# A buffer for each pair of heads for P's 512-column tiles, and three scratch tiles folded into others

## The reference

```
qkv    = xn @ w_qkv.T + b_qkv                 # 16 heads of 32
scores = q @ k.T / sqrt(32), causal           # 512 x 512 for each head
out    = softmax(scores) @ v                  # "AV"
attn   = out @ w_out.T + b_out
g, u   = (xn @ gate_w.T) * gate_s, (xn @ up_w.T) * up_s      # 1408 wide
ffn    = ((silu(g) * u) @ down_w.T) * down_s
```

## Time and profile before

| | |
|---|---|
| median of 3 runs | 1948.21 us (1943.7 to 1949.09) |
| the profiled execution | 1939.12 us |
| its span | 1937.2 us |
| granted TensorE clock | 0.993 |
| busy: PE / PEld / DVE / ACT / POOL | 96% / 63% / 78% / 74% / 65% |
| chain that ended last: PE / DVE / SP's queue / DMA / ACT | 66% / 9% / 8% / 7% / 5% |

### The profile page before, as it was taken

How to read it: one execution, slowest core, us unless ns; L and a number is a source line. 1 busy time by engine, 2 the same in 40 slices (tenths; PEclk the granted TensorE clock), 3 DMA queues, 4 the chain that set the end, 5 groups by cost and what they waited for, 6 DMA issues and landing times.

```text
span 1937.2 us, 44142 instructions
## 1 busy us (share of the span) xinstructions
PE 1864.4 (96%) x14978; PEld 1221.9 (63%) x14978; DVE 1503.4 (78%) x4516; ACT 1441.2 (74%) x4263; POOL 1255.9 (65%) x1799
## 2 busy tenths in 40 slices
PE   6899999999999999999999999999999999999996
PEld 4566665666666666675656666666566666766663
DVE  4878778787777878778777787877778777787785
ACT  4787777878777787777867778677687777778674
POOL 5775857757676675857748576575666656576462
PEclk9999999999999999999999999999999999999999
DMA  9978969788797977979789797887968778797685
GB/s 222 168 161 161 183 131 204 141 164 167 142 190 134 183 157 156 183 132 194 133 150 177 135 196 124 164 157 137 184 128 172 144 141 179 131 182 133 123 159 99
DMA packets 818551, 305.93 MB, mean 158 GB/s; under 512 B 756176, under 2 KB 793168, under 8 KB 818320
## 3 DMA queue, kind: packets, MB, share of 16 engines
q1 hardware_dynamic: 796176, 240.79, 69.3%
q0 software_dynamic: 22144, 62.27, 12.0%
HBM read 55.59 MB, written 16.78 MB: 37 GB/s over the span
## 4 chain that ended last, share of the span: by engine, by line
PE 66%; DVE 9%; SPq 8%; DMA 7%; ACT 5%; issue 3%; POOL 1%; POOLq 0%; ACTq 0%; DVEq 0%
PE bank L248 66%; DMA pt<-phl 6%; SPq L897 5%; DVE phl L552 3%; ACT phl L451 3%; SPq L904 2%; DVE bank L542 1%; ACT bank L459 1%; DVE res L579 1%; DVE small L516 1%; DVE xhl L692 1%; ACT small L447 0%; DVE ft L562 0%; SPq L889 0%; DVE fh L567 0%
## 5 line engine op out<-in xcount | busy, mean ns | idle before, releaser
L552 DVE SCALAR_TENSOR_TENSOR phl<-bank,small,phl 128x512 f16<-128x512 f32 (+3 forms) x1024 | 526.3, 545 | 200.3 <-ACT phl L451 197.4
L459 ACT ACTIVATE bank<-bank,small 128x512 f32<-128x512 f32 (+3 forms) x1024 | 516.0, 505 | 153.7 <-DVE small L542 152.9
L542 DVE CUSTOM_DVE_ANT_0 bank<-bank,mask 128x512 f32<-128x512 f32 (+3 forms) x1024 | 483.2, 503 | 146.0 <-PE bank L248 143.3
L451 ACT ACTIVATE phl<-bank,small 128x512 f16<-128x512 f32 (+3 forms) x1024 | 500.0, 531 | 110.7 <-DMA pt<-phl 100.3
L248 PE MATMUL bank<-xnT,wg 128*128 128x256 f16 x2816 | 367.6, 273 | 4.5 <-DVE fh L567 4.5
L248 PE MATMUL bank<-xnT,wu 128*128 128x256 f16 x2816 | 365.8, 273 | 0.0
L248 PE MATMUL bank<-xnT,wqkv 128*128 128x512 f16 x1536 | 352.4, 379 | 0.0
L248 PE MATMUL bank<-wd,ht 128*128 128x512 f16 x1408 | 316.1, 380 | 0.3 <-POOL ht L763 0.3
L248 PEld LDWEIGHTS bank<-xnT,wg 128*128 128x128 f16 x2816 | 263.9, 98 | 67.0 <-DVE fh L567 5.4
L248 PEld LDWEIGHTS bank<-xnT,wu 128*128 128x128 f16 x2816 | 276.0, 98 | 32.4
L248 PE MATMUL bank<-stk 96*128 96x512 f16 (+3 forms) x1024 | 245.6, 301 | 31.3 <-DVE phl L552 28.4
(11 more groups left out here) (97 smaller groups left out, 2181.7 us busy)
## 6 DMA issues: line engine op xcount, KB each, us to landing
stk<-qkp SPq DMA_DIRECT2D x768, 64.0 KB, 2.1
res<-in_x_dram POOLq DMA_DIRECT2D x64, 256.0 KB, 4.8
xin<-in_x_dram POOLq DMA_DIRECT2D x60, 256.0 KB, 4.7
out_dram<-res POOLq DMA_DIRECT2D x60, 256.0 KB, 3.4
pt<-phl SPq DMA_TRANSPOSE x512, 4.3
xin<-in_gate_dram POOLq DMA_DIRECT2D x11, 256.0 KB, 3.4
xin<-in_up_dram POOLq DMA_DIRECT2D x11, 256.0 KB, 3.4
xin<-in_down_dram POOLq DMA_DIRECT2D x11, 256.0 KB, 4.0
```

The lines of the kernel that those rows point to most:

```text
L451: i = eng.activation(phl[qt][:, j % 2, 0], pb[:, off:off + W], ACT.Copy, scale=st_r[:, c:c + 1])
L459: i = eng.activation(pb[:, off:off + W], pb[:, off:off + W], ACT.Exp, bias=st_m[:, c:c + 1], scale=-1.0, accum_out=st_s[:, c:c + 1])
L542: i = eng.tensor_tensor_reduce(out=bk[:, off:off + W], in0=bk[:, off:off + W], in1=mask[:, 512 - W:512], scale=-(32.0 ** -0.5) / (QS * QS) ...
L552: i = eng.scalar_tensor_tensor(phl[qt][:, j % 2, 1], pb[:, off:off + W], st_r[:, c:c + 1], phl[qt][:, j % 2, 0], ALU.mult, ALU.subtract)
```

## The change

It has three parts, and the order of every engine's work stays as it was but for the loads of x.

1. The 512-column size of `phl` gets a second tile, so that each pair has its own, with its own semaphore. `high` of a 512-column unit now waits for the turn of its own pair in the group before, and `av` waits on five landing semaphores instead of four.
2. `dtmp` becomes another name for `q32[0]`. `drain_av` additionally waits until every `down_add` ahead of it is done, `down_scale` until every `split_av` ahead of it is done.
3. `xs32` is gone: `scaled` normalises in place in `xin`. A buffer of `xin` is free for the next load only after the low half (L692) and no longer after `scaled`; the load is issued three steps ahead of the statistics (four for the one at step 3 of the first batch).

The second tile takes as many bytes of a partition (4096) as `dtmp` and `xs32` give back.

```diff
-    phl = [sb(f"phl{i}", [128, 2, 2, 128 * (i + 1)], F16) for i in range(4)]
+    phl = [[sb(f"phl{i}", [128, 2, 2, 128 * (i + 1)], F16)] for i in range(3)]
+    phl.append([sb(f"phl3_{p}", [128, 2, 2, 512], F16) for p in range(2)])
-    dtmp = sb("dtmp", [128, 512], F32)
+    dtmp = q32[0]
-    xs32 = sb("xs32", [128, 512], F32)
-    d_pt = [sem(f"d_pt{i}") for i in range(4)]
+    d_pt = [[sem(f"d_pt{i}")] for i in range(3)] + [[sem(f"d_pt3_{p}") for p in range(2)]]
+    avs_ahead = {bt: sum(n < m for n in av_at) for m, bt in d_at.items()}
+    ds_ahead = {G: sum(n < m for n in d_at) for m, G in av_at.items()}
-    later = [(n - 4, ("norm", *v)) for n, v in norm_at.items()] + ...
+    later = [(n - (4 if n < 4 else 3), ("norm", *v)) for n, v in norm_at.items()] + ...
-        xin_reader[i] = {"norm": (v_xs, 4 * what[1] + what[-1] + 1), ...
+        xin_reader[i] = {"norm": (v_xl, 4 * what[1] + what[-1] + 1), ...
+    part = lambda qt, j: phl[qt][j // 2 if qt == 3 else 0]
...
         def av(G):
-            for qt in range(4):
-                w.wait_ge(d_pt[qt], 16 * (2 * G + 2))
+            for qt in range(3):
+                w.wait_ge(d_pt[qt][0], 16 * (2 * G + 2))
+            for p in range(2):
+                w.wait_ge(d_pt[3][p], 16 * (G + 1))
...
         def drain_av(G):
             w.wait_ge(p_al, G)
+            w.wait_ge(p_dy, ds_ahead[G])
...
         def high(n):
             for j, qt, off in segs(u):
-                w.wait_ge(d_pt[qt], 16 * (2 * G + j // 2))
+                w.wait_ge(*((d_pt[3][j // 2], 16 * G) if qt == 3 else (d_pt[qt][0], 16 * (2 * G + j // 2))))
...
-        def scaled(i, t, xs, xi):
-            w.wait_ge(v_xl, i if i > 4 else 0)
+        def scaled(i, t, xi):
             w.wait_ge(p_rs, i + 1)
-            eng.tensor_scalar(xs, xi, st[:, 6:7], st[:, 8:9], ...).then_inc(v_xs, 1)
+            eng.tensor_scalar(xi, xi, st[:, 6:7], st[:, 8:9], ...).then_inc(v_xs, 1)
...
         def down_scale(b, t):
             w.wait_ge(p_dy, 4 * b + t)
+            w.wait_ge(p_al, avs_ahead[b, t])
...
         def turn_p(G, p, qt, n):
             eng.dma_start_transpose(pt[p][:, 12 * qt:12 * qt + nb, :],
-                                    phl[qt][:, :, :, :].rearrange("p a b c -> p (a b c)")).then_inc(d_pt[qt], 16)
+                                    part(qt, 2 * p)[:, :, :, :].rearrange("p a b c -> p (a b c)")).then_inc(d_pt[qt][p if qt == 3 else 0], 16)
```

More of the change, by code:

```diff
@@ L176, in fast_path @@
     xin_load_at, xin_turn, xin_free, xin_reader = {}, {}, {}, [None, None]
-    later = [(n - 4, ("norm", *v)) for n, v in norm_at.items()] + [(n - 3, ("check", c)) for n, c in check_at.items()]
+    later = [(n - (4 if n < 4 else 3), ("norm", *v)) for n, v in norm_at.items()] + [(n - 3, ("check", c)) for n, c in check_at.items()]
     for n, what in sorted(later + [(n - 3, ("wout", k)) for n, k in wout_at.items()]):
@@ L182, in fast_path @@
         xin_free[what] = xin_reader[i]
-        xin_reader[i] = {"norm": (v_xs, 4 * what[1] + what[-1] + 1), "check": (a_ms, what[1] + 1), "wout": (v_wo, what[1] + 1)}[what[0]]
+        xin_reader[i] = {"norm": (v_xl, 4 * what[1] + what[-1] + 1), "check": (a_ms, what[1] + 1), "wout": (v_wo, what[1] + 1)}[what[0]]
     res_at = {}
@@ L450, in high @@
                 c, W = 2 * (n % NSTAT) + k, 128 * (qt + 1)
-                i = eng.activation(phl[qt][:, j % 2, 0], pb[:, off:off + W], ACT.Copy, scale=st_r[:, c:c + 1])
+                i = eng.activation(part(qt, j)[:, j % 2, 0], pb[:, off:off + W], ACT.Copy, scale=st_r[:, c:c + 1])
             i.then_inc(a_hi, 1)
@@ L463, in scalar_program @@
         for t in range(4):
-            hl = xhl[t][:, 0] if t < 2 else phl[3][:, t - 2, 0]
+            hl = xhl[t][:, 0] if t < 2 else phl[3][0][:, t - 2, 0]
             w.wait_ge(v_xs, t + 1)
@@ L520, in statistics @@
             eng.tensor_scalar(st[:, 5:6], st[:, 7:8], EPS, 1.0 / (XS * XS), op0=ALU.add, op1=ALU.mult).then_inc(v_var, 1)
-        def scaled(i, t, xs, xi):
+        def scaled(i, t, xi):
             st = lst[t]
-            w.wait_ge(v_xl, i if i > 4 else 0)
             w.wait_ge(p_rs, i + 1)
-            eng.tensor_scalar(xs, xi, st[:, 6:7], st[:, 8:9], op0=ALU.subtract, op1=ALU.mult).then_inc(v_xs, 1)
+            eng.tensor_scalar(xi, xi, st[:, 6:7], st[:, 8:9], op0=ALU.subtract, op1=ALU.mult).then_inc(v_xs, 1)
         def reciprocals(n):
@@ L551, in low @@
                 c, W = 2 * (n % NSTAT) + k, 128 * (qt + 1)
-                i = eng.scalar_tensor_tensor(phl[qt][:, j % 2, 1], pb[:, off:off + W], st_r[:, c:c + 1], phl[qt][:, j % 2, 0],
+                i = eng.scalar_tensor_tensor(part(qt, j)[:, j % 2, 1], pb[:, off:off + W], st_r[:, c:c + 1], part(qt, j)[:, j % 2, 0],
                                              ALU.mult, ALU.subtract)
@@ L570, in v_low @@
             psum = job_bank["v", b, hf, tp][:, :].rearrange("p (a f) -> p a f", a=2)
-            part = lambda p: vv[:, p, 2 * tp:2 * tp + 2, 256 * hf:256 * hf + 256]
+            half_of = lambda p: vv[:, p, 2 * tp:2 * tp + 2, 256 * hf:256 * hf + 256]
             w.wait_ge(a_vh, 4 * b + 2 * hf + tp + 1)
-            eng.scalar_tensor_tensor(part(1), psum, QS / (XS * WS), part(0), ALU.mult, ALU.subtract).then_inc(v_vl, 1)
+            eng.scalar_tensor_tensor(half_of(1), psum, QS / (XS * WS), half_of(0), ALU.mult, ALU.subtract).then_inc(v_vl, 1)
         def out_add(b, t):
@@ L640, in first_low @@
         def first_low(t):
-            hl = xhl[t][:, :, :] if t < 2 else phl[3][:, t - 2]
+            hl = xhl[t][:, :, :] if t < 2 else phl[3][0][:, t - 2]
             w.wait_ge(a_xh, t + 1)
@@ L691, in vector_program @@
                 w.wait_ge(p_xh, 4 * b + t - 3)
-                eng.tensor_tensor(hl[:, 1], xs32[:, :], hl[:, 0], ALU.subtract).then_inc(v_xl, 1)
+                w.wait_ge(v_xs, 4 * b + t + 1)
+                eng.tensor_tensor(hl[:, 1], xin[t % 2][:, :], hl[:, 0], ALU.subtract).then_inc(v_xl, 1)
             if n - 2 in norm_at:
                 b, t = norm_at[n - 2]
-                scaled(4 * b + t, t, xs32[:, :], xin[t % 2][:, :])
+                scaled(4 * b + t, t, xin[t % 2][:, :])
             if n - 1 in wout_at:
@@ L863, in gpsimd_program @@
                 w.wait_ge(v_xs, i + 1)
-                eng.tensor_scalar(xhl[t % 2][:, 0], xs32[:, :], 1.0, 1.0, op0=ALU.mult, op1=ALU.mult).then_inc(p_xh, 1)
+                eng.tensor_scalar(xhl[t % 2][:, 0], xin[t % 2][:, :], 1.0, 1.0, op0=ALU.mult, op1=ALU.mult).then_inc(p_xh, 1)
             for i in ffn_load_at.get(n, ()):
@@ L914, in sync_program @@
         for t in range(4):
-            turn_x(0, t, xhl[t] if t < 2 else phl[3][:, t - 2])
+            turn_x(0, t, xhl[t] if t < 2 else phl[3][0][:, t - 2])
             load_weight(4 + t)
```

## The result

| | before | changed |
|---|---|---|
| median of the runs, us | 1944.24 (5 runs, 1942.73 to 1949.09) | 1931.75 (5 runs, 1921.9 to 1934.19) |
| profiled execution / its span, us | 1939.12 / 1937.2 | 1925.77 / 1922.4 |
| granted clock of the profiled execution | 0.993 | 0.996 |

The ratio is 0.9935, with a 95% interval of 0.991 to 0.996: 12.5 us faster by the medians, where 12.1 was forecast. The forecast time itself, 1936 us, is 4 us too high, mostly because it was counted from a median of three runs, 1948.21 us; that of five is 1944.24.

The account below looks back on a forecast made before the run. PE was taken as full inside its jobs, so only its holes could be won. Terms: -20.4 + 3.7 + 1.6 + 3 = -12.1 us, from 1948.2 to 1936 us; range 1925 to 1950.

Parts of the forecast that it names:

- PE's holes bound the kernel: PE is full inside its jobs, 0.216 us a matmul start; a change off PE can win only the holes between them.
- Rival C: ACT's loop, not PE, is the bound; half of 86.9 us returning gives 1905 us, all of it 1861; chance 0.03.
- The 20.4 us of holes: Second tile removes PE's holes: 18.1 us ahead of unit 9's scores, plus 2.28 us behind the output add; together 20.4 us.
- The other 2.3 us: PE's wait of 2.28 us behind the output add at 1008.74, following from a 4.08 us stall, counted as won.
- Unit 7 as the next wait, 3.7 us: ACT's wait partly moves to unit 7's high half, the 384-column size; 3.7 us of PE's gain are given back.
- grow by 2 to 4 us: Sign that the forecast is right: PE's waits ahead of the 512-column scores grow by 2 to 4 us.
- Rival A: The wait only moves to unit 7; 14.4 us given back instead of 3.7, total -1.4 us, 1947 us; chance 0.21.
- forecast 5.3: In group 13, ACT no longer late to unit 5 would wait 3.33 + 1.96 = 5.3 us at unit 7.
- Loads, 3 us: Loads of x one step later stand beside the turns unit 7 needs; 0.2 us a batch, 3 us cost.
- the extra wait of AV, 1.6 us: One more wait in PE's queue, 51 ns for each of 64 AVs; 0 to 3.3 us, middle taken, 1.6 us.
- The shared scratch, 0: Added waits of `drain_av` on ACT and `down_scale` on DVE have 5.97 and 7.65 us of room; cost 0.

Follow-up runs that it names:

- e2: Changed kernel with part 1 taken back: one 512-column tile for both pairs, parts 2 and 3 kept; 1944.84 us, ratio 1.0014 to the kernel before.
- e3: Changed kernel with second tiles for the 384- and 128-column sizes instead of the 512-column one, same bytes; 1948.60 us, ratio 1.0026 to the kernel before.
- e4: Changed kernel plus twelve small ACT instructions ahead of unit 5's high half in each batch's second group; 1938.93 us, ratio 0.9971 to the kernel before.
- e12: Changed kernel with x loads four steps ahead, gate/up products before AV in each batch's second group, later POOL bias additions; 1924.23 us, 0.9893 of the kernel before.
- e9_after: Changed kernel, unaltered, as the yardstick beside e11 and e12; 1931.06 us, ratio 0.9920 to the kernel before.
- e11: Changed kernel with POOL's four output-bias additions of a batch three steps later, from the second batch on; 1931.84 us, ratio 0.9932 to the kernel before.
- e1_after: Changed kernel, unaltered, as the yardstick beside e2, e3 and e4; 1931.16 us, ratio 0.9939 to the kernel before.

## Why the prediction was right, and where it was not

**PE's holes bound the kernel.** Right. e2 and e3 have the holes and no gain; e4 puts them back without any DMA and loses 7.8 us for 9.1 us of idle; e12 has 7.0 us less idle than e9_after and is 6.8 us faster by the medians. Rival C, ACT's loop as the bound, is out: in e3 and in the changed kernel ACT lost waits of 13 and of 87 us, and only those with a hole of PE behind them counted. The weight loads' busy share, by which the Trainium skill judges headroom ("Perfetto Trace Analysis", Identifying the Most-Contended Engine), is 63% in both kernels. By it a third of the span would be left to win; the gain had the size of the holes, and 87 us taken from ACT's waits gave no more.

**The 20.4 us of holes.** Right for the 18.1 us ahead of unit 9: 17.5 us of the 18.6 ahead of the 256-column scores went, and taking the tile back in e2 brought 11.9 of them again. The other 2.3 us, PE's wait behind the output add, are not shown to be the second tile's. That wait went from 3.8 to 0.6 us, but it is 0.6 in e2 and e3 too, where ACT stalls as before.

**Unit 7 as the next wait, 3.7 us.** The step failed for the changed kernel, in its place and in its size on ACT. I moved ACT's whole saving of 3.33 us forward to unit 7, as if nothing between could absorb it. The 3.7 us themselves came from the margins of three of the sixteen groups. The row maximum does: ACT's wait ahead of the 384-column exponentials rose by 62.8 us, from 72.9 to 135.7. The PE waits ahead of the 512-column scores did not grow by 2 to 4 us; those behind P's low half fell from 4.1 to 2.5 us. What took back part of the gain was a wait that the old holes had covered and that I had not looked for: POOL's hidden tile, 0.3 to 4.4 us, so 4.1 where I had 3.7. That sizes agree here is luck. The cover is shown: the wait is 4.2 to 4.8 us in the three executions of the changed kernel and at most 0.4 in e2, e3 and e4, which have the holes. Rival A in its form (the wait moves to unit 7 and costs 14.4 us) is out for the changed kernel. Its mechanism exists all the same: in e11 ACT waits 4.99 us ahead of unit 7 in group 13, where I had forecast 5.3, and PE 2.96 us behind it.

**Loads, 3 us, and the extra wait of AV, 1.6 us.** Neither is told from nothing. e2, which has the moved loads and the wait, is 0.8 us above the kernel before by the medians. PE's wait ahead of AV did grow by 1.7 us, from 7.8 to 9.5, and it was not uncovered by the holes that went, for it is 11.2 and 10.5 us in e2 and e3, which have them. But it varies from 7.4 to 11.2 us among the kernels that have AV in its old place, so whether the fifth semaphore, the loads or chance makes it longer is open. Another 1.3 to 2.0 us have nothing to do with PE: the time outside the span has a median of 1.6 to 2.0 us in the kernel before, by group of runs, and of 3.3 to 3.6 in every kernel with parts 2 and 3. I forecast no such term, and its cause is open.

**The shared scratch, 0.** Nothing contradicts it: neither `drain_av` nor `down_scale` waits for POOL in the lists of waits of ACT and DVE.

**The clock and the start.** Neither is in the forecast, so that the match of 12.1 and 12.5 us is partly luck. In the profiled pair 14.8 us of holes went between the start and the end (32.0 to 17.2), more than the 12.1 forecast in all. Ahead of 120 us 5.2 us came on top (25.0 to 30.2), most of it waits for DMAs. Whether the change makes the start longer is open: it moves three of the four loads of x that are issued there, but the new hole of 2.79 us at 107.02 is missing in e3 and e4, which have the moved loads too. The clock gave some back: ahead of 1900 us the kernel before has five stretches of 3.4 us at half clock and the changed one two, and three of them are worth 3 x 1.7 = 5.1 us. Three of the five, and one of the two, lie ahead of 120 us.

## What to carry to other kernels

- Where one engine is full, price a stall elsewhere by the hole that it leaves in the full engine (87 us on ACT were 18 us on PE), and confirm it by spending the same bytes on the neighbouring buffer: that took away a wait of ACT and gained nothing.
- A hole hides the waits that fall into it. Before counting a hole as won, ask of every other producer how late it would be for the very next job (POOL's tile, 0.3 us before, was 4.4 us late after); the list of waits shows only the last to come.
- Sum the idle of the full engine over the same work in both versions and compare sums, since single rows trade places from one version to the next. Between two fixed times the shorter version shows more of its end.

## What the runs showed of the hardware

The granted clock is not constant, and it falls beside PE's holes. In the kernel before, two of the falls stand behind holes of 2.06 us (ending at 913.9) and 2.28 us. Two rows of the profile for these stretches, with PE's clock third from the end:

```profile
914.50:917.90 3.40, 3.40 (x10) 1.18 (x8) 3.04 (x12) 3.37 (x12) 3.37 (x4) 0.50 1.09 189
1010.00:1013.40 3.40, 3.40 (x10) 1.30 (x9) 2.63 (x10) 1.88 (x7) 1.81 (x3) 0.51 1.10 233
```

For 3.4 us PE ran at half speed, the lower level of 1.2 GHz, and its twelve matmuls of 512 columns took 4.05 us where they take 2.75. In the changed kernel one fall between 100 and 1885 us is left, beside a hole of 2.79 us; its row, then the job in PE's timeline:

```profile
106.30:109.70 3.40, 2.68 (x7) 1.02 (x8) 2.77 (x8) 2.82 (x11) 3.19 (x4) 0.50 0.99 177
```

```profile
107.02 4.04 PE L252 MATMUL bank<-xnT,wqkv 128*128 128x512 f16 x12 [2.79 <-DMA xnT<-xhl]
```

Not every such hole is followed by a fall: those of 2.19 and 1.99 us at 123 and 443 us in the kernel before were not, nor was the one of 2.96 us at 457 us in e11. So a hole can cost its own length and, by an estimate from these rows, 1.3 us (4.05 less 2.75) to 1.7 us (half of 3.4) more. The spans follow the clock only in part: 1.9 us for each 0.001 in the 35 runs of the kernel before, 1.7 in the 12 of e1_after, whose mean clock is 0.0015 higher. That is some 3 of the 14 us between their mean spans, 1942.3 and 1928.1. The clock accounts for 38% of the variance of the spans among the 35 runs and for 47% among the 12; the rest of one kernel's spread is open.
